# A gated delta-rule layer on one core: the products of the chunk inverse taken in 64x64 quarters of the array

## The reference

```python
S_f = fdt * S_f;  S_s = sdt * S_s
S_f = S_f + bt * kt (vt - kt S_f);  S_s = S_s + bt * kt (vt - kt S_s)
S_fc = _cap(S_f + rf * S_s);  S_sc = _cap(S_s + rf * S_f)
ot = fgt * (qt S_fc) + sgt * (qt S_sc)
```

## Time and profile before

| | |
|---|---|
| Median of 3 runs | 3907.66 us (3900.67 to 3916.38) |
| Profiled execution | 3898.2 us, span 3896.0 us |
| TensorE matmul / weight load busy | 82% / 61% of the span |
| VectorE / ScalarE / POOL busy | 65% / 38% / 37% |
| Mean granted TensorE clock | 0.895 of full |
| Chunk loop | 1020 to 2872 us from the span's start |
| L915 matmuls (lower) | 433.8 us busy, 3072 of them |
| L925 matmuls (update) | 308.5 + 127.6 us busy, 3072 of them |

### The profile page before, as it was taken

How to read it: one execution, slowest core, us unless ns; L and a number is a source line. 1 busy time by engine, 2 the same in 40 slices (tenths; PEclk the granted TensorE clock), 3 DMA queues, 4 the chain that set the end, 5 groups by cost and what they waited for, 6 DMA issues and landing times. The chain is left out here.

```text
span 3896.0 us, 66300 instructions
## 1 busy us (share of the span) xinstructions
PE 3213.5 (82%) x23671; PEld 2387.0 (61%) x23671; DVE 2519.4 (65%) x4300; ACT 1493.2 (38%) x3143; POOL 1430.4 (37%) x2006
## 2 busy tenths in 40 slices
PE   0566997661599999999999999999958458999888
PEld 0444433551588888888888888888847345333334
DVE  8895777497147674676726666355549736777775
ACT  0234887441123332333323333233316245555554
POOL 0001776563244543454534554345536433000000
PEclk9777999776589997999969999799979779999999
DMA  1001555664212321322222232122218252111111
GB/s 27 0 1 66 221 219 220 137 165 137 55 35 53 75 56 32 75 56 70 38 66 38 59 75 56 44 59 55 61 56 292 58 160 58 17 26 18 25 17 30
DMA packets 434134, 293.20 MB, mean 75 GB/s; under 512 B 335100, under 2 KB 396092, under 8 KB 425022
## 3 DMA queue, kind: packets, MB, share of 16 engines
q1 hardware_dynamic: 418976, 263.98, 24.2%
q10 hardware_dynamic: 4608, 16.78, 1.4%
q0 software_dynamic: 10240, 8.41, 1.4%
HBM read 159.59 MB, written 129.45 MB: 74 GB/s over the span
## 5 line engine op out<-in xcount | busy, mean ns | idle before, releaser
L2328 DVE TENSOR_REDUCE mx<-banks 128x2 f32<-128x1024 f32 (+3 forms) x384 | 360.5, 956 | 149.8 <-PE banks L1799 110.3
L915 PE MATMUL banks<-xc,ssm 128*128 128x16 f32 (+2 forms) x3072 | 433.8, 283 | 13.9 <-issue 8.6
L915 PEld LDWEIGHTS banks<-xc,ssm 128*128 128x128 f32 x3072 | 395.9, 201 | 78.3 <-ACT ssm L1063 53.5
L2034 ACT ACTIVATE probs<-banks 128x1024 f32<-128x1024 f32 (+3 forms) x384 | 310.2, 811 | 286.6 <-PE banks L1821 156.3
L1072 ACT COPY xs<-banks 128x64 f32<-128x64 f32 (+2 forms) x384 | 109.0, 284 | 769.4 <-PE banks L915 769.4
L1555 POOL TENSOR_TENSOR prj_sq<-prj 128x1024 f32<-128x1024 f32 x64 | 218.3, 3430 | 389.0 <-ACT prj L1940 389.0
L925 PE MATMUL banks<-xs,ttw 128*128 128x32 f32 (+1 forms) x2048 | 308.5, 298 | 7.7 <-ACT xs L1072 7.7
L925 PEld LDWEIGHTS banks<-xs,ttw 128*128 128x128 f32 x2048 | 277.6, 210 | 39.2 <-ACT xs L1072 10.8
L1271 DVE SCALAR_TENSOR_TENSOR xc<-xc,halves,banks 128x64 f32<-128x64 f32 (+1 forms) x256 | 80.3, 314 | 336.1 <-PE banks L925 336.1
L794 POOL TENSOR_SCALAR xc<-xc,halves 128x64 f32<-128x64 f32 (+1 forms) x256 | 134.3, 525 | 428.0 <-DVE xc L1271 397.9
L1682 PE MATMUL banks<-wproj,xnT 128*128 128x512 f32 x512 | 266.4, 602 | 20.3 <-ACT prj L1940 19.4
(11 more groups left out here) (354 smaller groups left out, 7111.8 us busy)
## 6 DMA issues: line engine op xcount, KB each, us to landing
proj_s<-prj SPq DMA_DIRECT2D x32, 2048.0 KB, 6.3
qkv_t<-proj_s SPq DMA_DIRECT2D x32, 1536.0 KB, 6.6
ka<-proj_s ACTq DMA_DIRECT2D x32, 512.0 KB, 4.1
mem_s<-o_sb SPq DMA_DIRECT2D x32, 512.0 KB, 2.6
om<-mem_s SPq DMA_DIRECT2D x32, 512.0 KB, 3.8
om<-proj_s SPq DMA_DIRECT2D x32, 512.0 KB, 4.7
blk_s<-res SPq DMA_DIRECT2D x16, 512.0 KB, 4.6
rt_src<-r_s SPq DMA_DIRECT2D x512, 8.0 KB, 4.7
```

Of the source, the lines that this page charges most:

```text
L915: last = pe.matmul(products(k, lv)[:, w * m:w * m + w], ssm[:, lv, m, :], inverse_of(k, lv)[:, m, :], start=True, stop=True)
L2034: act.activation(probs[:, s % 2, :, at:at + w], slot_of((kind, s, k))[:, :, 0:w], ACT.Exp, scale=D1 ** -0.5).then_inc(b_read, 1)
L2328: dve.tensor_reduce(mx[:, s % 2, c, :, t:t + 1].rearrange("p e a -> p (e a)"), slot_of((kind, s, k))[:, :, 0:w], AX, ALU.max).then_inc(a_r ...
```

## The change

At the first two levels all blocks lie within the two diagonal 64x64 quarters, so each head's product becomes two products with 64x64 weights, one on rows and outputs 0 to 63, one on 64 to 127, into two different PSUM banks. At the last level only the quarter from rows 0 to 63 to outputs 64 to 127 is not zero, and one product with 64x64 weights is left. The copy to `xs` (ScalarE) and the update (VectorE) of levels 0 and 1 become two operations of 64 partitions each. At the last level VectorE only writes the negated lower left quarter, and POOL copies the upper left quarter from xc2 ahead of its old operation. Products and semaphore counts at the end of each run stay as they were.

```diff
+        HALVES = (slice(0, 64), slice(64, 128))
+        def quarters(lv):
+            return [(0, HALVES[0], HALVES[1])] if lv == LEVELS - 1 else [(b, HALVES[b], HALVES[b]) for b in range(2)]
-        def products(k, lv):
+        def products(k, lv, b):
             at = (0, 0, 256)[lv]
-            return slot4(k)[3 if lv == 0 else 0][:, at:at + 4 * (SUB << lv)]
+            return slot4(k)[3 - b if lv == 0 else b][:, at:at + 4 * (SUB << lv)]
...
+                if lv == LEVELS - 1:
+                    pool.tensor_copy(tw[0:64, k % 2, :, 0:w], xc2[0:64, k % 2, :, :])
                 pool.tensor_scalar(inverse_of(k, lv + 1)[:, :, w:2 * w], inverse_of(k, lv), halves[:, lv, 1:2], None, ALU.mult).then_inc(half_set, 1)
...
-                    last = pe.matmul(products(k, lv)[:, w * m:w * m + w], ssm[:, lv, m, :], inverse_of(k, lv)[:, m, :], start=True, stop=True)
+                    for out_, rows, right in quarters(lv):
+                        last = pe.matmul(products(k, lv, out_)[right, w * m:w * m + w], ssm[rows, lv, m, right], inverse_of(k, lv)[rows, m, :], start=True, stop=True)
...
-                    last = pe.matmul(updates(k, lv)[:, w * m:w * m + w], turned, xs[:, k % 2, w * m:w * m + w], start=True, stop=True)
+                    for out_, rows, right in quarters(lv):
+                        last = pe.matmul(updates(k, lv, out_)[right, w * m:w * m + w], turned[right, right], xs[right, k % 2, w * m:w * m + w], start=True, stop=True)
...
-                act.copy(xs[:, k % 2, 0:4 * (SUB << lv)], products(k, lv)).then_inc(x_set[lv], 1)
+                for out_, rows, right in quarters(lv):
+                    last = act.copy(xs[right, k % 2, 0:4 * (SUB << lv)], products(k, lv, out_)[right, :])
+                last.then_inc(x_set[lv], 1)
...
-                dve.scalar_tensor_tensor(out=inverse_of(k, lv + 1)[:, :, 0:w], in0=inverse_of(k, lv), scalar=halves[:, lv, 0:1],
-                                         in1=updates(k, lv).rearrange("p (h t) -> p h t", t=w), op0=ALU.mult, op1=ALU.subtract).then_inc(tw_set[lv], 1)
+                for out_, rows, right in quarters(lv):
+                    new_ = updates(k, lv, out_)[right, :].rearrange("p (h t) -> p h t", t=w)
+                    if lv == LEVELS - 1:
+                        last = dve.tensor_scalar(tw[right, k % 2, :, 0:w], new_, -1.0, None, ALU.mult)
+                    else:
+                        last = dve.scalar_tensor_tensor(out=inverse_of(k, lv + 1)[right, :, 0:w], in0=inverse_of(k, lv)[right, :, :], scalar=halves[right, lv, 0:1],
+                                                        in1=new_, op0=ALU.mult, op1=ALU.subtract)
+                last.then_inc(tw_set[lv], 1)
```

More of the change, by code:

```diff
@@ L616, in slot4, with updates @@
             return bank[4 * (k % 2):4 * (k % 2) + 4]
-        def products(k, lv):
+        HALVES = (slice(0, 64), slice(64, 128))
+        def quarters(lv):
+            return [(0, HALVES[0], HALVES[1])] if lv == LEVELS - 1 else [(b, HALVES[b], HALVES[b]) for b in range(2)]
+        def products(k, lv, b):
             at = (0, 0, 256)[lv]
-            return slot4(k)[3 if lv == 0 else 0][:, at:at + 4 * (SUB << lv)]
-        def updates(k, lv):
+            return slot4(k)[3 - b if lv == 0 else b][:, at:at + 4 * (SUB << lv)]
+        def updates(k, lv, b):
             at = (64, 128, 0)[lv]
-            return slot4(k)[3 if lv == 0 else 0][:, at:at + 4 * (SUB << lv)]
+            return slot4(k)[3 - b if lv == 0 else b][:, at:at + 4 * (SUB << lv)]
         def span4(k, first_bank, banks_):
```

## The result

| | before | changed |
|---|---|---|
| Median, first measurement | 3912.01 us | 3809.34 us |
| Ratio, 95% interval | | 0.9746 (0.9715 to 0.9777) |
| Profiled execution, span | 3896.0 us | 3794.8 us |
| Mean granted clock | 0.895 | 0.884 |
| From the first to the last solve | 1846.4 us | 1752.6 us |

The change saves 2.5%, where 174 us or 4.5% were forecast. Beside the later experiments, on another chip, the same kernel had a ratio of 0.9743 (0.9704 to 0.9783).

The account below looks back on a forecast made before the run. TensorE bounds the kernel through mostly zero weight loads, with VectorE's last update as second limit. 110 steps x 1.36 = 150, less 17, plus 41, saves 174 us: 3898.2 to 3724, plus 9.5, gives 3733; range 3690 to 3790.

Parts of the forecast that it names:

- the rival of dear hand-overs: Draining quarters or semaphores behind two-piece copies cost 0.15 us more at each of six places: 3830 us; 12%.
- the signs given: If right: solve to solve 12.2 to 12.4 us, clock 0.99, lower 0's 16 loads about 0.55, answers 1.0 to 1.1.
- The price of a quarter pair: TensorE's loads of two diagonal 64x64 quarters overlap: 0.055 us per pair at full clock, bounds 0.055 and 0.11.
- the rival of no overlap: Diagonal quarters load in series, runs of levels 0 and 1 last 1.0 instead of 0.57 us: 3963 us; 8%.
- The price of changing shape: TensorE, last load to next run's first: 0.18 us after quarter runs, 0.31 or 0.26 after full ones.
- States 0: TensorE run ahead of lower 2: 0.88 us instead of 0.65, a new wait of 0.24 for both VectorE pieces.
- Factors and solve: Factors, ahead of the solve: 0.89 us instead of 0.70, from VectorE's 2.2 us of work between its updates.
- Nothing of it is on the path: POOL's extra copy, priced at 0.40 us, delays only POOL's own work, with some 0.4 us of slack left.
- a rival of all or nothing: Clock falls in the long stretches, all 110 steps going at 17.25 us: 4300 us; 8%.
- Inverse rows: On some 24 steps VectorE's block inverse rows start lower 1 about 0.7 us later: 17 us taken off the saving.
- The slow steps at first chunks: 18 half-clock steps at the sequences' first chunks each save 2.3 us: 41 us.
- the rival in which the clock rises: At first chunks, 18 slow steps fall from about 18 to 12 us, 110 us more off: 3620 us; 10%.

Follow-up runs that it names:

- e7: Changed kernel plus two unused full products ahead of each solve, with POOL's upper left quarter copy made by ScalarE instead; 0.9597 of the kernel before.
- e5: Changed kernel with VectorE's state product moved from ahead of the level 2 update to behind it; 0.9550 of the kernel before.
- e3: Changed kernel with two more full products, whose results nothing reads, ahead of each solve; 0.9611 of the kernel before.
- e4: Kernel before the change with one more VectorE fill, about 1.3 us, ahead of the level 2 update; 1.0656 of the kernel before.
- e1: Changed kernel with levels 0 and 1 back to full 128x128 products, only level 2 a quarter; 1.0432 of the kernel before.
- e10: Changed kernel with state product behind level 2 update, two unused products ahead of solves at first chunks only, block inverse begun a step earlier; 0.9361 of before.
- e12: Changed kernel unaltered, measured again on another chip beside the kernel before; 0.9743 of the kernel before.

## Why the prediction was right and where it was not

The direction and the prices of the quarters held. The forecast of 3733 was 76 us low (3809): outside its own range of 3690 to 3790 and inside the wider one of 3610 to 3850, but the upper end of that was set by the rival of dear hand-overs, which did not happen. Of the signs given, the loads and the answers came out right; the step was 12.67 and not 12.2 to 12.4, and the clock in the long stretches 0.92 to 0.96 and not 0.99.

On the traces 174 us were forecast and 101 came. Missing are 67 us of the clock, 39 of a step that is longer than forecast and 3 for two steps that were counted too many; made good are the 17 held back for inverse rows (what they cost is in the other counts), 12 at the first chunks and 7 in the rest of the program, which the sum did not have. The last two are luck.

- *The price of a quarter pair*, 0.055: 0.058 (15 intervals of 0.029 between matmuls of a run). Right, so the rival of no overlap is out.
- *The price of changing shape*: answers 1.09 and values 1.03 for 1.09 and 1.04, quarter runs 0.57 to 0.59. Right; the new boundaries cost what the old ones had shown (the rule of the Trainium skill, TensorEngine Tiling (Array Packing), section Key Properties, that a change of mode drains the engine, agrees). The rival of dear hand-overs is out.
- *States 0*, a new wait for VectorE's two pieces: 0.95 for 0.88, and the pieces took 0.71 for 0.70. Right in kind, though the row ahead of lower 2 says "issue" and doesn't name VectorE; lower 2 starts 0.07 behind the end of the pieces (2206.35).
- *Factors and solve*: this term was mis-sized. I took VectorE's 2.2 us between its two updates from the old trace. They became 2.56 (2206.35 to 2208.91): 0.26 more in the state product and 0.08 in the output operation ahead of it (0.50 for 0.42). With POOL's copy taken away (e7) the same stretch is 2.23 (2209.14 to 2211.37). So the sentence on POOL that failed is "Nothing of it is on the path": its copy was costed for POOL's own path only, not for what POOL's later work does to VectorE beside it. The step is 12.67 and not 12.30: 0.26 more ahead of the solve, 0.07 in states 0 and 0.03 at the turn, about 40 us over the long stretches. e5 removes the bound and gives 12.17.
- *The clock*: the larger miss. I priced its fall as a rival of all or nothing, every step of the long stretches at 17.25, at 8%, and took it as zero in the sum. It falls in 46 of 108 steps, mostly for 3.4 us, and costs 1.6 us in each. I held the streamed columns against it, the same in a shorter step, and did not look at where the new waits lie: 0.6 us right ahead of the solve, behind the part of the step with the small products. 67 us. That the wait lets it fall is shown by e3, which fills it, and by e4, which makes one with full products; e1 shows that falls can also begin elsewhere, for a reason that stays open.
- *Inverse rows*, 17 us: right in kind. They delay the 12 steps at the starts of the six inverses and not 24; the one first step that kept the clock took 13.44, 0.77 above the others, for 0.7 forecast. Most took 14.8 to 15.2, because the clock then falls too; e10 gets most of that back.
- *The slow steps at first chunks*: 41 us forecast for 18, 53 measured for 19 (14.8 to 29.3 us each before, a wider spread than the 17.25 to 21.36 read). The clock there is up more of the time (188 us at 1.2 GHz instead of 253), but in the second trace of the changed kernel (e12) it is 235 us and the gain 35, so the surplus over 41 is not shown, nor is the rival in which the clock rises.

## What to carry to other kernels

Packing small products by quarters pays as the loads of rows and column halves in the old trace say, and each change of tile shape costs 0.1 to 0.2 us that can be read there too. Once TensorE is no longer the only bound, look at what now ends its waits, and at where they lie: in e4 a wait of 0.84 us more cost 89 us by itself and 161 more through the clock. An operation given to an engine with time to spare can also lengthen another engine's work beside it: look at what then runs at the same time. Then reorder the engine that is late, or fill only the waits that reordering cannot remove; a filling product where TensorE doesn't wait costs its full time.

## What was not expected of the hardware

- A wait of 0.84 us more per step ahead of the solve (1.01 for 0.17), all products unchanged, dropped the clock in 60 of 108 steps (e4), and products of no use that filled such a wait made the program 1.4% faster (e3). In the stretch of e1 shown above the clock fell for 10.2 us right behind 20 us in which TensorE was busy for 98%.
- The half of the change with the least new in it (e1) was 4.3% slower than nothing, while the other half gained 1.9% and both together 2.5%: the parts don't add.
- One VectorE operation of 128x256 on SBUF took 425 ns with nothing of POOL beside it, and the same beside one of POOL's small operations of the bound (e5); it took 0.74 us beside 0.46 us of POOL's square and 1.00 us beside all 0.61 of it. Why the square does that no run here shows.
